# The transfer that puts the maxima's rows into the stacks, issued by GpSimd instead of ScalarE

## The reference

```
xq, xk, xv = x @ wq.T, x @ wk.T, x @ wv.T        # (4, 256, 32, 16) each
xq, xk = rotary(xq), rotary(xk)
scores = einsum('bqhd,bkhd->bhqk', xq, xk) * 16 ** -0.5
scores = where(causal, scores, -1e30)
x = layernorm(x + (softmax(scores) @ xv) @ wo.T)
gate, up = (x / 128) @ w_gate.T, (x / 128) @ w_up.T     # 1376 wide
q = trunc(clip(silu(gate) * up * 128, -128, 127))
x = layernorm(x + trunc(clip((q @ w_down.T) * 128, -128, 127)))
```

## Time and profile before

| engine | busy us | share of the span | instructions |
|---|---|---|---|
| PE (matmul) | 371.6 | 93% | 2532 |
| DVE | 256.7 | 64% | 902 |
| ACT | 218.7 | 54% | 417 |
| POOL | 83.9 | 21% | 80 |

### The profile page before, as it was taken

The page is one execution under the profiler, slowest core; times in us unless marked ns, Lnnn a source line. Parts: engine busy times, 40 slices in busy tenths (PEclk is TensorE's granted clock), DMA queues, the critical chain, the costliest instruction groups (busy, mean ns, idle before and its releaser), DMA issues.

```text
span 401.6 us, 7269 instructions
## 1 busy us (share of the span) xinstructions
PE 371.6 (93%) x2532; PEld 286.4 (71%) x2532; DVE 256.7 (64%) x902; ACT 218.7 (54%) x417; POOL 83.9 (21%) x80
## 2 busy tenths in 40 slices
PE   7987987999889998988999998899999999999991
PEld 4765755777667776765776776688888888878880
DVE  5767776665666766588444446766555555548886
ACT  5785486766837758587554542454433344333331
POOL 4022022201122002250220001135023333111111
PEclk9999898999999999999999999899999999999997
DMA  8867939367470773937910400014022201001111
GB/s 277 319 129 157 154 78 154 65 138 113 79 140 7 123 155 60 225 63 159 209 58 7 159 0 0 8 46 158 2 78 78 78 26 27 0 2 52 53 54 52
DMA packets 79842, 37.61 MB, mean 94 GB/s; under 512 B 68672, under 2 KB 72896, under 8 KB 79808
## 3 DMA queue, kind: packets, MB, share of 16 engines
q1 hardware_dynamic: 76928, 35.08, 37.8%
q10 hardware_dynamic: 2880, 2.10, 2.6%
HBM read 17.24 MB, written 2.10 MB: 48 GB/s over the span
## 4 chain that ended last, share of the span: by engine, by line
PE 71%; DVE 7%; ACT 6%; DMA 5%; SPq 5%; issue 4%; POOL 1%; ACTq 1%; POOLq 0%; DVEq 0%
PE bank L836 6%; PE bank L838 5%; PE bank L837 5%; PE bank L978 5%; PE s_pair L836 5%; PE s_pair L838 5%; PE s_pair L837 5%; PE st_pair L838 4%; PE st_pair L836 4%; PE st_pair L837 4%; PE bank L1075 4%; PE bank L1076 4%; SPq L237 3%; PE st_pair L960 3%; DMA XR<-xT 3%
## 5 line engine op out<-in xcount | busy, mean ns | idle before, releaser
L635 DVE CUSTOM_DVE_ANT_0 SM<-s_pair,K 128x128 bf16<-128x128 f32 (+1 forms) x256 | 76.1, 353 | 54.3 <-PE s_pair L947 54.1
L423 ACT ACTIVATE PTS<-st_pair 128x384 f32<-128x384 f32 x128 | 56.1, 492 | 39.5 <-PE st_pair L963 34.2
L319 POOL TENSOR_TENSOR RQ<-RQ,QS 128x256 f32<-128x256 f32 x32 | 22.2, 693 | 119.2 <-ACT QS L402 119.1
L549 ACT ACTIVATE f_a<-f_c 128x512 f32<-128x512 f32 x22 | 13.9, 632 | 58.5 <-DVE f_c L765 58.5
L304 POOL TENSOR_TENSOR GL<-gu_raw,GH 128x1024 fp32r<-128x1024 f32 x11 | 26.9, 2446 | 80.3 <-ACT GH L466 80.3
L960 PE MATMUL st_pair<-identb,maskb 128*128 128x256 bf16 x128 | 35.9, 280 | 6.2 <-ACT PTS L423 6.1
L836 PE MATMUL bank<-WQH,XH 128*128 128x512 f32 x88 | 38.5, 437 | 0.0
L837 PE MATMUL bank<-WQL,XH 128*128 128x512 f32 x88 | 35.2, 400 | 0.0
L838 PE MATMUL bank<-WQH,XL 128*128 128x512 f32 x88 | 35.2, 399 | 0.0
L1075 PE MATMUL bank<-DH,IQ 128*128 128x512 f32 x88 | 34.4, 390 | 0.2 <-POOL DL L309 0.2
L1076 PE MATMUL bank<-DL,IQ 128*128 128x512 f32 x88 | 34.2, 389 | 0.0
(11 more groups left out here) (122 smaller groups left out, 865.0 us busy)
## 6 DMA issues: line engine op xcount, KB each, us to landing
gu_raw<-wgu SPq DMA_DIRECT2D x11, 512.0 KB, 4.5
w_raw<-wqkvo SPq DMA_DIRECT2D x6, 512.0 KB, 8.8
wd_raw<-wd SPq DMA_DIRECT2D x11, 256.0 KB, 3.1
RES<-x SPq DMA_DIRECT2D x4, 512.0 KB, 4.2
out<-o SPq DMA_DIRECT2D x8, 256.0 KB, 2.0
XR<-xT SPq DMA_DIRECT2D x3, 512.0 KB, 4.3
w_raw<-wqkvo ACTq DMA_DIRECT2D x4, 256.0 KB, 4.5
QT<-QS SPq DMA_TRANSPOSE x64, 3.6
```

The costliest lines, as they stand in the source:

```text
L423: nc.scalar.activation(PTS[:, (2 * p + half) % R_PTS, :], st_pair[:, half, 0:SW], ACT.Exp, scale=-1.0).then_inc(S["pr"], 1)
L635: last = nc.vector.tensor_tensor_reduce(out=SM[:, half, cols], in0=s_pair[:, half, cols], in1=above, scale=1.0, scalar=HUGE, op0=ALU.add, ...
```

## The change

The wait and the transfer of `max_out` leave ScalarE. GpSimd gets a function `max_rows` with the same wait, the same transfer and the same semaphores, called at the head of the same step.

```diff
+            def max_rows(g):
+
+                pool.wait_ge(S["mt_c"], g + 1)
+                pool.dma_start(QT[g % OCTS][SROWS:MROWS, 0, :, :],
+                               MT[0:2 * OCT, g % 2, :].rearrange("p (o t) -> p o t", o=1).broadcast_to((2 * OCT, OCT, T))).then_inc(S[f"mq{g % 2}"], 16)
+
             for m in range(4):
                 rest(0, 0, m)
             for g in range(STEPS):
                 b, s = divmod(g, PAIRS)
+                if LAG_M <= g <= NP + 1 and (g - LAG_M) % 4 == 0:
+                    max_rows((g - LAG_M) // 4)
...
                 nc.scalar.activation(MT[0:2 * OCT, g % 2, :], bAV[0:2 * OCT, T:T + P].bitcast(BF16), ACT.Copy).then_inc(S["mt_c"], 1)
-                act.wait_ge(S["mt_c"], g + 1)
-                act.dma_start(QT[g % OCTS][SROWS:MROWS, 0, :, :],
-                              MT[0:2 * OCT, g % 2, :].rearrange("p (o t) -> p o t", o=1).broadcast_to((2 * OCT, OCT, T))).then_inc(S[f"mq{g % 2}"], 16)
```

## The result

The changed kernel is slower. Median 408.55 us (406.07 to 411.10, 15 runs) against 406.24 us (402.44 to 410.31, 15 runs) of the kernel before on the same chip; ratio 1.0066, 95% interval 1.0041 to 1.0092, or +2.7 us (1.7 to 3.7). The forecast was 404.9 us beside a median of 405.21 us for the kernel before, that is no measurable change. The profiled execution took 407.78 us, its span 406.0.

What follows compares the result with a forecast made beforehand. TensorE was taken as the bound in most of the attention, with short stretches waiting on ScalarE or SyncE's queue. Gains of 2.52 against losses of 2.20 gave net -0.3 us: 404.9 us on the medians' scale, range 402.5 to 408.7.

Steps and rivals of the forecast that it cites:

- Chain at 44 us, -0.65: SyncE's transposing transfer at 44.36 us, held by ScalarE's issue through a shared generator, gets 0.65 us shorter.
- relief: Where transposes are issued beside it, the transfer of the maxima lands 0.65 us sooner, no longer queued behind them.
- no relief: Rival: generator not shared, so the 0.65 us gains do not come; +2.8 us, 408.0 us; chance 0.15.
- Group 14, -0.47: Transfer issued at 207.24 us: TensorE's 0.47 us idling at 211.51 for OH and OL goes.
- Group 6, -0.70: Transfer issued at 107.87 us: exponentials and copies 0.70 us earlier, all taken from TensorE's 1.01 us last wait.
- Group 10, -0.70: Transfer issued at 159.21 us: 0.70 us gained from 1.15 of idling; landing at 163.16, TensorE comes at 163.28.
- Group 13, +1.23: Transfer issued at 194.31 us: GpSimd busy with GL, issue 2.17 us later, landing 200.23, used at 199.00.
- Groups 2, 8 and 12: Transfers issued at 61.68, 134.70 and 183.51 us: later landings cost TensorE 0.28, 0.24 and 0.45 us.
- the other twelve: Remaining ScalarE issues, in stretches where TensorE or the stacks end last: removing them gains 0.
- x = 1.0: Estimate that GpSimd's transfer lands 1.0 us later than ScalarE's issued at the same moment, before any relief.
- quick-issue rival: Rival: GpSimd's transfer lands only 0 to 0.4 us later; at 0.4, -2.2 us, 403.0 us; chance 0.18.
- The signs of being wrong: Median landing over 1.5 us beyond 3.2, no transfer waited for, or GpSimd's subtraction L319 making ScalarE wait.

Runs made afterwards that it cites:

- e_sp: All 16 transfers issued by SyncE, each between two transposing transfers, instead of by ScalarE as in the kernel before; ratio 1.0012.
- e_late610: Kernel before, ScalarE issuing all, but the transfers near 108 and 159 us issued between the two exponentials; ratio 1.0003.
- e_only13: Kernel before with only the transfer near 194 us issued by GpSimd, behind its weight part GL; ratio 1.0069.
- e_gl: Changed kernel with GpSimd's weight part GL of steps 56 and 60 one step later, behind the transfer; ratio 1.0005.
- e_only6: Kernel before with only the transfer near 108 us issued by GpSimd, the other 15 by ScalarE; ratio 1.0000.

## Why the prediction was wrong

- **Chain at 44 us, -0.65: false.** The step was that ScalarE's issue holds up SyncE's queue through a shared generator. ScalarE issues nothing there now, and SyncE's long row is still there, 2.13 beside 1.33 (it was 1.99 beside 1.34). The row of 1.99 could not have waited for ScalarE's issue in the first place: that issue ran from 42.28 for 0.73 us, and the row began at 44.36. What makes the row long is open. It comes with the transfer from ScalarE and from GpSimd alike, and in e_sp, where SyncE issues it, the transposes' rows next to the transfers of groups 0, 6, 10 and 12 are 1.23 to 1.41 us. With the step falls the "relief" of 0.65 in the landings. Of the rivals, "no relief" had this part: group 13 cost 2.03, where it had 1.88. That its +2.8 us is also the measured 2.7 is luck: it has 0.89 for group 8 and 0.53 for group 10, where 0.24 and 1.47 came, and a gain of 0.47 at group 14 that never came.
- **Group 14, -0.47: false.** The wait for OL kept its 0.47, as group 6's kept its 1.00. At group 14 TensorE had no wait for PTS, ScalarE's exponentials came 0.65 us sooner behind the copy, and nothing moved. At group 6 TensorE and OL both came 0.8 us early and the wait between them stayed. So what ends the wait for OL isn't what stood behind ScalarE's issue. I had read two waits in a row as one that holds the whole gain.
- **Group 6, -0.70: right in size**, -0.81 to -0.84, but by luck: it came from the wait for PTS, which I had not read, and not from that for OL, on which the term was built.
- **Group 10, -0.70 "with 0.12 to spare": wrong.** The gain of 0.98 came and 1.47 was paid at 164 us. The step that failed is that a landing stays where it was when TensorE comes early. In the kernel before the landing is at 3.65 us behind the copy, in the changed kernel at 5.35, and with ScalarE as the issuer it was 5.28 too (e_late610). TensorE's own instruction fetch came early with it and met the transfer's end; how far that is the whole reason is open, as said above. No rival had this.
- **Group 13, +1.23: mechanism right, size off**, 2.03. GpSimd was busy with GL as forecast (2.15 us from the copy to the issue against 2.17). The landing took 4.53 from its issue, where the working had 3.4 + 1.0 - 0.65 = 3.75. That is the term that was mis-sized: it took the landing of an earlier moment, ahead of the loads of 512 and 256 KB (under e_only13).
- **Groups 2, 8 and 12**, +0.28, +0.24, +0.45: about +0.5, +0.24 and +0.15. Group 12's small error is two that cancel: a gain of 0.65 at PTS, counted at nothing among "the other twelve", and a cost of 0.80 for the transfer because TensorE came early, where 0.45 was forecast. x = 1.0 was too large where nothing else runs: groups 1, 11, 12 and 15 land 0.15 to 0.30 us later than before, by the copy's end. With transposes beside it (groups 0, 2, 6, 8) it is 0.3 to 0.5. The relief, wrong as it was, hid the first error in the sum. One figure of the quick-issue rival is wrong by its own working: at x = 0.4 the transfer of 183.51 lands 0.07 us after its use and not 0.18; nothing hangs on it.
- **Sum.** -0.3 became +2.6: 0.65 (relief) + 0.47 (group 14) + 1.19 (group 10) + 0.80 (group 13) + 0.2 (group 2) - 0.3 (group 12) - 0.1 (group 6). The timing resolves the whole and, by e_gl and e_only13, the part of group 13. The terms of the other groups stand on profiles alone.
- **The signs of being wrong** named beforehand did not show: the median landing, from the end of the copy, grew from 3.23 to 3.81 us, transfers were waited for, ScalarE's waits for GpSimd's subtraction stayed at 2 us in all, and the exponentials started within 0.1 us of the copy in 14 of the 16 groups. These signs could not catch this error, because it lay in single groups and not in the median.

No version beats both kernels: e_gl and e_only6 equal the kernel before. The gains of 0.8 and 1.0 us are real in the traces; the one that would keep both needs group 10's fetch elsewhere, and the two ways tried to move it cost more than it gives.

## What to carry to other kernels

Before moving an issue to another engine, look at what that engine does in the microsecond of each of the issues: one of 16 behind a 2.4 us instruction decided the verdict. Subtract a gain only at the wait that the changed step ends, and only where the next thing has slack of its own. If a landing has under 2 us of slack (the late ones here were 1.4 to 2.1 us late), look for an instruction packet between its issue and its end, and where it goes when the engine is earlier.

## What the runs showed of the hardware that I had not expected

- A 16 KB instruction packet that starts 0.6 to 3.4 us behind the copy goes with one late landing of the 16 in 28 of 40 transfers (in the changed kernel's group 10, 15 in by 3.73 us and the last at 5.35), against 1 of 248 without one.
- Satisfied waits on TensorE start 106 ns apart: 60 of them turned 1.01 us of idling into 5.77. Yet leaving out 101 of them made the kernel 0.9% slower.
- A transfer's last landing among transposes came 0.5 to 0.85 us later in five groups and 0.11 in a sixth when 8 KB more were written beside it.
- An issue of SyncE that is 0.65 to 0.8 us longer than its neighbours is no sign that it waited for ScalarE's issue: it stayed (2.13 beside 1.33) when ScalarE issued nothing.
